# A gated cross-attention and expert-choice block: sorting half rows on 64 lanes, and another order of the routing tiles

## The reference, cut to what matters

```
kv = (ctx @ W_kv.T + b_kv).reshape(B, S, 16, 16, 2); k, v = kv[..., 0], kv[..., 1]
scores  = einsum('bshd,bstd->bsht', layernorm(x) as heads, k) / 4
context = einsum('bsht,bstd->bshd', softmax(scores), v)
x = x + tanh(g_xattn) * (context @ W_out.T + b_out)

probs = softmax(einsum('ntd,ed->nte', layernorm(x), gate_w))
g, m  = top_k(probs.transpose(0, 2, 1), 64)        # per batch element and expert
h     = gelu(xin[m] @ w1[e]) @ w2[e]               # hidden size 1024
x = x + tanh(g_ffn) * scatter_add(m, g * h)
```

## Time and profile before

| what | value |
|---|---|
| median of 3 runs | 736.58 us (736.11 to 738.33) |
| profiled execution, its own time | 736.63 us |
| its span, first to last instruction | 734.6 us |
| PE (TensorE matmul) busy | 641.7 us, 87% |
| DVE busy | 619.9 us, 84% |
| POOL busy | 550.1 us, 75% |
| ACT busy | 434.1 us, 59% |
| mean granted TensorE clock | 0.928 of full |

### The profile page before, as it was taken

One profiled execution on the slowest core, in us unless ns is written; L12 is line 12 of the kernel. 1 busy time (PEld: TensorE's weight loads), 2 busy tenths in 40 slices (PEclk: granted clock), 3 DMA queues, 4 the chain that ended last, 5 costly groups with the idle time before them and its releaser, 6 DMA issues.

```text
span 734.6 us, 10843 instructions
## 1 busy us (share of the span) xinstructions
PE 641.7 (87%) x3592; PEld 514.2 (70%) x3592; DVE 619.9 (84%) x726; ACT 434.1 (59%) x1077; POOL 550.1 (75%) x497
## 2 busy tenths in 40 slices
PE   5668786654799999997999999979999999999994
PEld 2334333322678888775888888758888889999994
DVE  4999999999999999889999999899999461577762
ACT  5477767643577777855777777657776533233320
POOL 3888888888868888698888887888888625445534
PEclk9988898655699999998999999989999999999997
DMA  6967774322367778766887777577777868999972
GB/s 177 345 231 259 263 242 188 125 99 75 123 182 247 237 230 231 224 201 175 243 237 230 230 237 231 185 218 206 235 229 219 268 174 271 317 308 314 308 217 29
DMA packets 97068, 160.90 MB, mean 219 GB/s; under 512 B 8171, under 2 KB 74486, under 8 KB 97014
## 3 DMA queue, kind: packets, MB, share of 16 engines
q1 hardware_dynamic: 84150, 142.91, 58.9%
q0 software_dynamic: 12288, 16.79, 12.1%
q10 hardware_dynamic: 576, 0.52, 0.2%
HBM read 126.63 MB, written 33.55 MB: 218 GB/s over the span
## 4 chain that ended last, share of the span: by engine, by line
PE 55%; DVE 21%; DMA 9%; issue 7%; POOL 6%; ACT 2%; POOLq 0%; ACTq 0%; DVEq 0%
PE bank L1017 20%; PE bank L998 20%; DVE prod_v L459 9%; DMA out_dram<-ys,ids 7%; DVE co L461 5%; PE bank L925 5%; DVE S L461 4%; PE bank L945 3%; POOL prod_p L313 2%; PE bank L986 2%; PE bank L908 2%; DMA xg<-xn_scratch,ids 1%; POOL tree_a L319 1%; POOL out_dram L379 1%; PE bank L957 1%
## 5 line engine op out<-in xcount | busy, mean ns | idle before, releaser
L998 PE MATMUL bank<-xin,w1in 128*128 128x256 f32 x1536 | 206.4, 292 | 7.6 <-issue 4.7
L998 PEld LDWEIGHTS bank<-xin,w1in 128*128 128x128 f32 x1536 | 195.8, 198 | 9.1 <-issue 8.7
L1017 PE MATMUL bank<-w2s,hT 128*128 128x256 f32 x768 | 175.4, 382 | 0.0
L379 POOL DMA_INDIRECT out_dram<-ys,ids x64 | 110.0, 1719 | 76.2 <-ACT ys L748 57.8
L1017 PEld LDWEIGHTS bank<-w2s,hT 128*128 128x128 f32 x768 | 142.4, 190 | 17.8
L738 ACT ACTIVATE hT<-bank 128x512 f32<-128x512 f32 x128 | 76.5, 598 | 117.9 <-PE bank L998 117.5
L461 DVE TENSOR_REDUCE co<-prod_v 128x208 f32<-128x3328 f32 (+2 forms) x32 | 109.7, 3428 | 1.1
L459 DVE TENSOR_TENSOR prod_v<-bank,Ex 128x3328 f32<-128x3328 f32 (+2 forms) x32 | 109.5, 3423 | 0.1
L313 POOL TENSOR_TENSOR prod_p<-kvs,q 128x1024 f32<-128x1024 f32 (+2 forms) x32 | 94.6, 2955 | 14.5 <-ACT q L706 14.5
L459 DVE TENSOR_TENSOR prod_v<-bank,q 128x3072 f32<-128x3072 f32 (+2 forms) x32 | 98.1, 3066 | 6.6 <-ACT q L706 6.6
L461 DVE TENSOR_REDUCE S<-prod_v 128x192 f32<-128x3072 f32 (+2 forms) x32 | 98.2, 3070 | 1.1
(11 more groups left out here) (123 smaller groups left out, 1079.9 us busy)
## 6 DMA issues: line engine op xcount, KB each, us to landing
w1in<-w_parts SPq DMA_DIRECT2D x128, 512.0 KB, 5.6
w2s<-in_L_ffn_w_dram SPq DMA_DIRECT2D x32, 1024.0 KB, 6.1
w_parts<-w1s SPq DMA_DIRECT2D x32, 512.0 KB, 3.5
w1raw<-in_L_ffn_w_dram SPq DMA_DIRECT2D x32, 256.0 KB, 4.4
ct<-in_ctx_dram SPq DMA_DIRECT2D x32, 128.0 KB, 4.5
xt<-in_x_dram SPq DMA_DIRECT2D x32, 128.0 KB, 4.6
out_dram<-x SPq DMA_DIRECT2D x32, 128.0 KB, 4.3
xn_scratch<-xn SPq DMA_DIRECT2D x32, 128.0 KB, 2.8
```

Of the source, the lines that this page charges most:

```text
L379: pool.indirect_dma_start(out=out_rows[:, :], out_offset=bass.IndirectOffsetOnAxis(ap=ids[:, g % 2, p * E + e:p * E + e + 1], axis=0), in_ ...
L998: ins = pe.matmul(HB[k % 2][:, D * f:D * (f + 1)], w1in[:, k, w, c, P * f:P * (f + 1)].bitcast(f32r), xin[:, n % 2, x_, c, :], start=(m == ...
L1017: ins = pe.matmul(dst, hT[:, n % 2, f, cols], w2s[:, n % 2, f, :], start=(f == 0), stop=(f == FC - 1))
```

## The change

The sort works on 64 rows (half row j, batch element, expert) of 128 tokens instead of 32 rows of 256. `pr` is transposed in one piece. Each half row gives its own 64 best in falling order. lists_out merges the two lists of a row: the late half's list is moved to lanes 0 to 31 and read backwards, and of each pair (earlier half's i-th, later half's (63 - i)-th) the larger probability is taken, with its index chosen by a comparison. Those 64 winners are the 64 best of the whole row, in another order. The other part is order: in routing tiles POOL issues `rsqrt` behind the product of its scores instead of in front of it; ACT makes q of a routing tile behind x_stats, loads Exp and does gate_exp in front of x2_stats in the tile before, and in the routing tile makes q, warms Exp and does the exponentials in front of gelu 2 and 3; x2_stats comes before take_y; TensorE does route_columns between hidden 2 and hidden 3. New buffers and semaphores are left out below.

```diff
+    R2 = J * R0
-        work = sb("work", [R0, T])
-        top_p = sb("top_p", [R0, CAP])
-        top_i = sb("top_i", [R0, CAP], u32)
+        work = sb("work", [R2, P])
+        top_p = sb("top_p", [R2, CAP])
+        top_i = sb("top_i", [R2, CAP], u32)
...
         # POOL
-            def share(heads, in0, in1, dst, n_tree, done):
+            def share(heads, in0, in1, dst, n_tree, done, root=None):
...
                 pool.tensor_tensor(pv, in0, in1, ALU.mult).then_inc(prodp_s, 1)
+                if root is not None:
+                    rsqrt(root)
                 pool.wait_ge(prodp_s, n_tree + 1)
...
-                share(H - hk, Kv, qi, S[:, hk * DK:H * DK], 2 * t, Sp_done)
+                share(H - hk, Kv, qi, S[:, hk * DK:H * DK], 2 * t, Sp_done, t + 1 if routing(t) else None)
...
             for s in range(NT):
-                if routing(s):
-                    rsqrt(s + 1)
                 scores(s)
...
         # DVE
-                dve.tensor_copy(work[:, :], XT[0:R0, 0:T]).then_inc(work_ready, 1)
+                dve.tensor_copy(work[:, :], XT[0:R2, 0:P]).then_inc(work_ready, 1)
...
             def lists_out(g):
-                for v, src in enumerate((top_i, top_p)):
-                    dve.tensor_copy(lists2[:, v], src[:, :].unsqueeze(1).broadcast_to([R0, 2, CAP])).then_inc(lists_ready, 1)
+                twice = lambda m: m.unsqueeze(1).broadcast_to([R0, 2, CAP])
+                backward = lambda m: m[:, ::-1]
+                dve.tensor_copy(top_f[:, :], top_i[:, :]).then_inc(index_cast, 1)
+                dve.tensor_copy(late_p[:, :], top_p[R0:R2, :]).then_inc(late_moved, 1)
+                dve.wait_ge(index_cast, g + 1)
+                dve.tensor_scalar(late_f[:, :], top_f[R0:R2, :], float(P), None, ALU.add).then_inc(late_moved, 1)
+                dve.wait_ge(late_moved, 2 * g + 1)
+                dve.tensor_tensor(earlier[:, :], top_p[0:R0, :], backward(late_p), ALU.is_ge).then_inc(earlier_set, 1)
+                dve.wait_ge(late_moved, 2 * g + 2)
+                dve.tensor_tensor(id_gap[:, :], top_f[0:R0, :], backward(late_f), ALU.subtract).then_inc(gap_made, 1)
+                dve.tensor_tensor(lists2[:, 1], twice(top_p[0:R0, :]), twice(backward(late_p)), ALU.max).then_inc(lists_ready, 1)
+                dve.wait_ge(earlier_set, g + 1)
+                dve.wait_ge(gap_made, g + 1)
+                dve.tensor_tensor(id_gap[:, :], id_gap[:, :], earlier[:, :], ALU.mult).then_inc(gap_kept, 1)
+                dve.wait_ge(gap_kept, g + 1)
+                dve.tensor_tensor(lists2[:, 0], twice(id_gap[:, :]), twice(backward(late_f)), ALU.add).then_inc(lists_ready, 1)
...
         # ACT, tiles 0 to 9
+                if routing(s + 1):
+                    gate_exp(s // TG - 1)
                 take_ctT(s + 2)
                 if s >= 1:
                     x2_stats(s - 1)
-                if routing(s + 1):
-                    gate_exp(s // TG - 1)
         # ACT, routing tile
                     x_stats(s + 2)
+                    make_q(s + 1)
+                    act.activation(exp_warm[:, :], tanh_g[:, 0:1], ACT.Exp)
                     take_xnT(s - 2)
+                    exponentials(s)
                     if n >= 0:
                         gelu(n, 2)
                         gelu(n, 3)
                     take_logits(s - 2)
-                    make_q(s + 1)
-                    act.activation(exp_warm[:, :], tanh_g[:, 0:1], ACT.Exp)
-                    exponentials(s)
+                    x2_stats(s - 1)
                     if n >= 1:
                         take_y(n - 1)
-                    x2_stats(s - 1)
                     take_xh(n + 1)
         # ACT, other tiles
                     x_stats(s + 2)
+                if routing(s + 1):
+                    make_q(s + 1)
                 take_xnT(s - 2)
                 gelu(n, 2)
                 gelu(n, 3)
                 take_logits(s - 2)
-                if s + 1 < NT:
+                if routing(s + 1):
+                    act.activation(exp_warm[:, :], tanh_g[:, 0:1], ACT.Exp)
+                    gate_exp(s // TG - 1)
+                elif s + 1 < NT:
                     make_q(s + 1)
                 x2_stats(s - 1)
-                if routing(s + 1):
-                    gate_exp(s // TG - 1)
                 if n >= 1:
                     take_y(n - 1)
...
         # TensorE
-                for j in range(J):
-                    ins = pe.transpose(XT[0:R0, P * j:P * (j + 1)], pr[:, j, :, :].rearrange("p b e -> p (b e)"), ident[:, :])
-                ins.then_inc(prT_psum, 1)
+                pe.transpose(XT[0:R2, 0:P], pr[:, :, :, :].rearrange("p j b e -> p (j b e)"), ident[:, :]).then_inc(prT_psum, 1)
...
                 if n >= 0:
                     hidden(n, 2)
+                if routing(s):
+                    route_columns(s // TG - 1)
+                if n >= 0:
                     hidden(n, 3)
                 logits(s - 2)
-                if routing(s):
-                    route_columns(s // TG - 1)
```

More of the change, by code:

```diff
@@ L129, in flamingo_gated_block_kernel @@
         pr = sb("pr", [P, J, BG, E])
-        work = sb("work", [R0, T])
-        top_p = sb("top_p", [R0, CAP])
-        top_i = sb("top_i", [R0, CAP], u32)
+        work = sb("work", [R2, P])
+        top_p = sb("top_p", [R2, CAP])
+        top_i = sb("top_i", [R2, CAP], u32)
+        top_f = sb("top_f", [R2, CAP])
+        late_p = sb("late_p", [R0, CAP])
+        late_f = sb("late_f", [R0, CAP])
+        earlier = sb("earlier", [R0, CAP])
+        id_gap = sb("id_gap", [R0, CAP])
         lists2 = sb("lists2", [R0, 2, 2, CAP])
@@ L178, in flamingo_gated_block_kernel @@
         route_psum, ids_ready, gts_ready = sem("route_psum"), sem("ids_ready"), sem("gts_ready")
+        index_cast, late_moved, earlier_set, gap_made, gap_kept = (
+            sem("index_cast"), sem("late_moved"), sem("earlier_set"), sem("gap_made"), sem("gap_kept"))
         xg_loaded, xt_psum, xh_ready, xin_ready = (
```

## The result

The changed kernel took **725.76 us** (median of 4, 725.46 to 725.87) against 737.46 for the kernel before (4 runs, 736.11 to 740.34; the 736.58 that the forecast starts from is the median of the three lower ones): ratio **0.9836, 95% interval 0.9804 to 0.9867**. The profiled execution has a span of 723.8 us where before had 734.6, thus 10.8 less; the forecast's sum was 12.4.

What follows compares the result with a forecast made beforehand. Three chains, on DVE, POOL and ACT, were taken to delay the hidden layer behind routing tiles. Gains of 0.8 + 4.6 + 4.6 + 1.5 + 0.9 = 12.4 us off 736.6 gave 724.2, range 720.5 to 731.5.

Steps and rivals of the forecast that it cites:

- The waits of tiles 18 and 26: Behind each of these routing tiles, the reordering and shorter sort start the next hidden 4.6 us earlier.
- The sort: DVE's token choice in routing tiles: 24 instructions on 128 columns save 3.2 us, and lists_out adds 1.6.
- The clock: TensorE's hole before hidden shrinks from 6.7 to 3.5 us, so two thirds return: 1.5 in tile 18, 0.9 in 26.
- TensorE keeps what it won: In ordinary tiles DVE has 1.0 us to spare each, so it catches up with the clock's 2.4 and nothing is lost.
- Tile 10 and the shared port: In tile 10 the row maximum waits for POOL, gaining 0.8 us; port conflicts between DVE and POOL are taken as nothing.
- The tail: In the last group TensorE is busy throughout at full clock, so the sort is hidden whole: gain 0.
- 1 (no shrinking): Sort instructions do not shorten with fewer columns, so route_columns waits 2.1 us: 732.4, chance 0.08.
- 2 (late gather): The gather moves into the w1 loads and needs 2.5 us more, delaying hidden: 731.6, chance 0.11.
- 5 (gain given back): q, rs or pr is held by something unforeseen, with another 4 us wait in each tile: 736, chance 0.08.
- 3: DVE's lists_out is held behind POOL's scatters at the shared port, TensorE waiting 1.9 us: 730.3, chance 0.07.
- 4 (TensorE stands at route_columns): Lists come late, so TensorE waits 3.6 us in the midst of its work and its clock falls: 742.4, chance 0.06.

Runs made afterwards that it cites:

- sort_only: The changed kernel with every engine's order as in the kernel before, keeping the new sort and merge: 739.76 us, ratio 1.0028 to the kernel before.
- rsqrt_front: The changed kernel with POOL's rsqrt put back in front of the scores of a routing tile: 738.84 us, ratio 1.0013 to the kernel before.
- again: The changed kernel run once more with no edit: 725.79 us, ratio 0.9856 to the kernel before.
- lists_in_psum: The changed kernel with the merge's held operands (top_f, late_p, id_gap) moved from SBUF to PSUM: 725.39 us, ratio 0.9842 to the kernel before.
- busy_psum: The changed kernel with eleven filler matmuls before hidden in tile 12 and behind tiles 18 and 26, and lists_out's intermediates in PSUM: 721.89 us.
- gate_back: The changed kernel with gate_exp behind x2_stats again and without its Exp warm-up: 729.90 us, ratio 0.9900 to the kernel before.
- order_only: The changed kernel's new engine order with the old sort on 32 rows of 256 tokens: 728.62 us, ratio 0.9889 to the kernel before.

## Why the prediction was right

724.2 was forecast and 725.76 measured, inside 720.5 to 731.5, and faster by more than 0.3%. (The lower end, redone from its own terms, is 720.8: 1.3 for the rest of the clock and 0.7 in each of three lists_out.) The mechanism was right in the two tiles that carry the gain. The smaller terms were off both ways and partly cancel: against 12.4 the profiled span has 0.7 more in the waits, 1.4 less in the clock, 1.5 less before tile 18, 0.5 less in the ordinary tiles and an unforecast 1.2 more in the tail, thus 10.8. That they add up to so little is in part luck. Step by step:

- **The waits of tiles 18 and 26: 4.6 each, measured 4.93 and 4.93.** The rows are where the working put them: `q` early, POOL without its 5.10, `pr` before TensorE, no wait at route_columns, `den` without its 1.36, DVE's 0.4 for the columns (0.33).
- **The sort: 3.2 less, list building 1.6 more.** From the copy to the row maximum it takes 9.49 us (312.13 to 321.62) instead of 11.21 (313.74 to 324.95): 1.72 net, forecast 1.6. Its worth depends on the rest: 2.8 us on top of the new order, a loss of 2.8 without it. The forecast said that POOL stood close behind; sort_only and rsqrt_front show that it decides.
- **The clock: 1.5 and 0.9 added, measured 2.30 and -1.33,** together 0.97 instead of 2.4. "The hole shrinks from 6.7 to 3.5, two thirds come back" took the hole's length as the cause of a set price. `again` shows the stretches change places at about the same holes. Counted the same way, what comes back against the one profile of before is 2.2 in `again` and 0.75 in lists_in_psum: 1.3 in the mean of the three, so the term was too large by about one.
- **"TensorE keeps what it won" held in part.** Of the 2.30 in tile 18, 0.50 went in the ordinary tiles behind (106.38 instead of 105.88), where TensorE once waits 0.28 for `xn`; in `again`, which had no such lead, they take 105.88. DVE's spare 1.0 for each tile was counted, but not the way over `x`, `rs` and `xn`. What the rest of the 0.50 is no row shows.

```profile
360.64 0.44 PE L933 MATMUL bank<-ident,xn 128*128 128x128 f32 x2 [0.28 <-ACT xn L737]
```

- **Tile 10 and the shared port: 0.8, measured -0.69.** The working had the row maximum wait for POOL, with the port at nothing. POOL's scores did end 0.88 earlier (175.27 instead of 176.15), but lists_out was held beside POOL's additions, so the row maximum began 0.65 behind them and gained only 0.45. lists_in_psum and busy_psum put the cost of the hold at 0.75. The rest of the miss is the clock: a slow stretch came out from behind DVE's wait.
- **The tail: 0, measured 1.16.** In the last 14.60 us of both spans TensorE is busy 7.05 at a granted clock of 0.75 before, and 6.23 at 0.84 after. Up to there the two kernels keep the same distance (9.70 at 676.03 and 666.33). So this is the clock again and no part of the change.
- **The rivals.** 1 (no shrinking), 2 (late gather) and 5 (gain given back) did not come: 281 ns, a wait of 0.88, 7.23 and 3.60 kept. 3 is the interesting one: its mechanism is real. The Trainium skill (SBUF — State Buffer, section Who interferes with whom) says that a DVE instruction with two SBUF inputs and a POOL instruction that reads SBUF exclude each other whole, and that cast and tensor_scalar, too, can take the shared pair of ports. The trace of tile 10 agrees: the difference, with two inputs in SBUF, takes 0.52 us instead of 0.20 in the tail, the cast 0.73 instead of 0.18. In tile 18 it nearly came to nothing because POOL's additions end 0.9 before lists_out begins; rsqrt_front shows what it looks like if they don't. One thing went otherwise than the forecast had it: DVE was held by POOL's additions and hardly by the scatters that it named. The cast at 319.94 began beside a scatter of 319.21 to 320.82 and took 0.37, and in gate_back a shift beside one took 0.47 instead of 0.17, so 0.2 to 0.3 each. 4 (TensorE stands at route_columns) is what order_only and rsqrt_front run into, with 0.76 and 3.12.

## What to carry to other kernels

Here two engines' chains ended close together, and the shorter sort alone brought nothing: the order of the second chain had to be mended first, and each half measured alone showed which pays. A wait that an in-order engine meets in front of a long instruction belongs behind it, if its reader is late anyway; here one such line, put back beside the other moves, cost 13 us. Price a fall of the clock as a mean over executions, not per place, and where TensorE has a hole that cannot be closed, a few matmuls without a reader in it are cheap to try. Before a trace is taken to say that something is free, count from an event of the same execution: times from the start of the span differed by 0.76 between two executions here, as much as the effect looked for.

## What the hardware showed that was not expected

- Behind equal holes (0.88 and 1.59 us) TensorE runs 24 matmuls in 3.11 or in 5.46, in one and the same execution. In the next execution of the same program the places are changed, 4.60 and 3.11, and in lists_in_psum both take 4.60. Eleven matmuls in the hole kept the full rate at all three places in both profiles with them.
- Some short DVE instructions end together with the POOL addition beside them: a cast of 64x64 takes 0.18 us in the tail, 0.73 in tile 10, 1.83 in rsqrt_front, and 0.21 with its output in PSUM. The copy of 32x64 behind it took 0.18 in tile 10 too, but it began with POOL's next addition (both 173.73), so the rows don't tell whether a copy is never held or came first.
- A backward read costs nothing that shows. On 32 lanes and 64 columns, in the tail, the two merges that read backwards (L571, L573) take 0.21 and 0.20 us and the forward product (L577) 0.20.
- MAX8, FIND_INDEX8 and MATCH_REPLACE8 take 281, 277 and 268 ns on 64 lanes and 128 columns, and 410, 406 and 397 on 32 lanes and 256 columns: as many elements in all, yet less time with fewer columns.
